# An attention and coupling block on one core: the softmax scale moved into the f16 split of q and k

## What is computed

```
x = x + layernorm(attention(layernorm(x)))
x = x + layernorm(coupling_cycles(layernorm(x)))        # 3 cycles of a small network with gelus

# attention: 16 heads of width 64, segments of 128 rows, carried memory M and normaliser Z
scores  = (q @ k.T) * (1 / sqrt(64))                    # per head and segment, 128 x 128
scores  = where(upper triangle, -inf, scores)
att_dot = softmax(scores) @ v
att_mem = (elu(q) + 1) @ M / ((elu(q) + 1) @ Z.T)
M, Z    = M + (elu(k) + 1).T @ v,  Z + sum(elu(k) + 1)
out     = (gate * att_mem + (1 - gate) * att_dot) @ Wo
```

## Time and profile before

| | |
|---|---|
| median of three runs | 1298.55 us |
| lowest and highest | 1297.96, 1299.42 us |
| profiled execution, first to last instruction (span) | 1296.2 us |
| TensorE matmul, busy | 1091.5 us, 84% |
| VectorE, busy | 913.4 us, 70% |
| ScalarE, busy | 596.7 us, 46% |
| POOL (GpSimd), busy | 582.6 us, 45% |
| mean granted clock of TensorE | 0.946 |

### The profile page before, as it was taken

One profiled execution on the slowest core, in us unless ns is written; L12 is line 12 of the kernel. 1 busy time (PEld: TensorE's weight loads), 2 busy tenths in 40 slices (PEclk: granted clock), 3 DMA queues, 4 the chain that ended last, 5 costly groups with the idle time before them and its releaser, 6 DMA issues.

```text
span 1296.2 us, 20762 instructions
## 1 busy us (share of the span) xinstructions
PE 1091.5 (84%) x7108; PEld 764.7 (59%) x7172; DVE 913.4 (70%) x1668; ACT 596.7 (46%) x1255; POOL 582.6 (45%) x715
## 2 busy tenths in 40 slices
PE   3798889886989898878888888798989779999992
PEld 1476657564767575647676756576767665433431
DVE  4868686876686868657878786868686754444486
ACT  4344444544454444443535354445444543444463
POOL 2145454544454545434545454545454552222274
PEclk9899999988899999989999999989999888999996
DMA  5000000000000000000000000000000010300033
GB/s 159 20 9 9 10 9 11 8 14 6 10 9 9 9 9 10 10 10 10 9 9 9 9 10 9 9 9 9 9 1 9 1 28 1 138 0 0 1 65 65
DMA packets 14681, 24.00 MB, mean 19 GB/s; under 512 B 5104, under 2 KB 6896, under 8 KB 14064
## 3 DMA queue, kind: packets, MB, share of 16 engines
q1 hardware_dynamic: 14576, 22.63, 5.7%
HBM read 13.97 MB, written 8.65 MB: 17 GB/s over the span
## 4 chain that ended last, share of the span: by engine, by line
PE 41%; DVE 38%; issue 11%; ACT 6%; POOL 2%; DMA 1%; DVEq 1%; SPq 0%; POOLq 0%; ACTq 0%
DVE arena L769 10%; PE ps L1172 9%; PE ps L1067 8%; PE ps L1278 6%; DVE arena L867 3%; PE ps L1125 3%; DVE arena L788 3%; ACT arena L555 3%; PE ps L1291 3%; DVE arena L819 2%; PE ps L1112 2%; DVE arena L713 2%; DVE arena L801 2%; DVE arena L779 2%; DVE arena L782 2%
## 5 line engine op out<-in xcount | busy, mean ns | idle before, releaser
L1067 PE MATMUL ps<-arena 128*128 128x512 f16 x1152 | 270.8, 386 | 6.0 <-DVE arena L745 4.2
L555 ACT ACTIVATE arena<-ps,arena 128x128 f32<-128x128 f32 x512 | 140.7, 381 | 252.4 <-DVE arena L791 251.3
L769 DVE STREAM_TRANSPOSE arena<-ps 128x1024 f32<-128x1024 f32 x96 | 189.8, 1979 | 35.4 <-PE ps L1067 35.4
L1067 PEld LDWEIGHTS ps<-arena 128*128 128x128 f16 x1152 | 113.1, 100 | 129.4 <-issue 14.0
L402 POOL TENSOR_TENSOR arena<-arena 128x256 f32<-128x256 f32 x128 | 93.1, 728 | 153.3 <-DVE arena L801 153.3
L1125 PEld LDWEIGHTS ps<-arena 128*128 128x128 f32 x1024 | 135.7, 202 | 29.5 <-issue 21.2
L1125 PE MATMUL ps<-arena 128*128 128x65 f32 x1024 | 139.2, 281 | 16.2 <-DVE arena L801 15.0
L386 POOL TENSOR_TENSOR arena<-arena 128x512 f32<-128x512 f32 x64 | 81.2, 1268 | 135.4 <-ACT arena L548 135.2
L1112 PE MATMUL ps<-arena 128*128 128x128 f32 x512 | 84.5, 303 | 45.6 <-ACT arena L555 45.5
L1172 PE MATMUL ps<-arena 128*128 128x256 f32 x544 | 122.0, 382 | 0.3 <-ACT arena L567 0.3
L372 POOL TENSOR_TENSOR arena<-arena 128x2 f32<-128x2 f32 x50 | 9.8, 196 | 230.8 <-DVE arena L709 230.8
(11 more groups left out here) (110 smaller groups left out, 1920.9 us busy)
## 6 DMA issues: line engine op xcount, KB each, us to landing
x_rows<-arena SPq DMA_DIRECT2D x17, 256.0 KB, 2.0
arena<-in_L_attn_x_dram SPq DMA_DIRECT2D x64, 64.0 KB
arena<-x_rows SPq DMA_DIRECT2D x4, 1024.0 KB, 7.9
out_dram<-arena SPq DMA_DIRECT2D x32, 128.0 KB, 2.9
arena<-in_L_attn_Wq_dram SPq DMA_DIRECT2D x1, 1024.0 KB, 12.3
arena<-in_L_attn_Wk_dram SPq DMA_DIRECT2D x1, 1024.0 KB, 14.4
arena<-in_L_attn_Wv_dram SPq DMA_DIRECT2D x1, 1024.0 KB, 17.4
arena<-in_L_attn_Wo_dram SPq DMA_DIRECT2D x1, 1024.0 KB, 13.0
```

The source lines that it names most:

```text
L555: last = act.activation(Pr[:, par, j, :], s_bank[:, par, j * P:(j + 1) * P], ACT.Exp, scale=SCALE, bias=shift[:, par, j:j + 1])
L769: dve.transpose(dst[:, d0:d0 + 32, :], bank.rearrange("p w (d c) -> p d w c", c=C)).then_inc(x_free, 1)
L1067: last = pe.matmul(bank[:, w, :], xc[:, lx, k, w * P:(w + 1) * P], W16[lw][:, k, i, :], start=(n == 0), stop=(n == 5))
```

## The change

The scale 1/8 is applied as 1/2 on q and 1/4 on k where they are split into f16 parts. The copies of the high parts get the factor as their scale. The subtractions of the low parts become T * factor - high, as `scalar_tensor_tensor`. The scores then come scaled out of TensorE. The multiply of L791, its buffer `shift` and the wait before it go away, the exponential has no scale but its default and takes `negm` as its bias, and `m_done` counts two signals for each group. elu(q)+1 is made from the unscaled q as before.

```diff
-SCALE = DK ** -0.5
+Q_SCALE, K_SCALE = 0.5, 0.25
+assert Q_SCALE * K_SCALE == DK ** -0.5
...
-        shift = alloc(GU).rearrange("p (h j) -> p h j", h=2)
...
-                    act.activation(qhT[g % 2].rearrange("p j i -> p (j i)"), t_bank[b], ACT.Copy).then_inc(qk_act, 1)
+                    act.activation(qhT[g % 2].rearrange("p j i -> p (j i)"), t_bank[b], ACT.Copy,
+                                   scale=Q_SCALE).then_inc(qk_act, 1)
...
-                    act.activation(khT[g % 2].rearrange("p j i -> p (j i)"), t_bank[b], ACT.Copy).then_inc(qk_act, 1)
+                    act.activation(khT[g % 2].rearrange("p j i -> p (j i)"), t_bank[b], ACT.Copy,
+                                   scale=K_SCALE).then_inc(qk_act, 1)
...
-                        act.wait_ge(m_done, bp * 64 + (4 * G + 2 * par + 2))
+                        act.wait_ge(m_done, bp * 32 + (2 * G + par + 1))
                         for j in range(GP):
                             last = act.activation(Pr[:, par, j, :], s_bank[:, par, j * P:(j + 1) * P], ACT.Exp,
-                                                  scale=SCALE, bias=shift[:, par, j:j + 1])
+                                                  bias=negm[:, par, j:j + 1])
...
-                    dve.tensor_tensor(f(qlT[g % 2]), T, f(qhT[g % 2]), ALU.subtract).then_inc(t_free[b], 1)
+                    dve.scalar_tensor_tensor(f(qlT[g % 2]), T, Q_SCALE, f(qhT[g % 2]), ALU.mult,
+                                         ALU.subtract).then_inc(t_free[b], 1)
...
-                    dve.tensor_tensor(f(klT[g % 2]), t_bank[b], f(khT[g % 2]), ALU.subtract).then_inc(t_free[b], 1)
+                    dve.scalar_tensor_tensor(f(klT[g % 2]), t_bank[b], K_SCALE, f(khT[g % 2]), ALU.mult,
+                                         ALU.subtract).then_inc(t_free[b], 1)
...
-                        dve.wait_ge(m_done, bp * 64 + (4 * G + 2 * par + 1))
-                        dve.tensor_scalar(shift[:, par, :], negm[:, par, :], SCALE, None,
-                                          ALU.mult).then_inc(m_done, 1)
```

## The result

The changed kernel takes 1285.86 us (median; 1283.12 to 1286.9) against 1298.26 us of the kernel before on the same chip: a ratio of 0.9896, interval 0.9878 to 0.9915. It is faster by 12.4 us (11.0 to 15.8 by the interval); the forecast was 17.7. The profiled execution took 1285.42 us, with a span of 1283.6 us where it was 1296.2.

What follows compares the result with a forecast made beforehand. It took the attention stage to be bound by a path changing between TensorE and VectorE. Groups 0, 3 and 2 gave 9.2 + 4.3 + 4.2 = 17.7 us off, forecasting 1281 us, range 1274 to 1288 (1271 to 1291 with neighbours).

Steps and rivals of the forecast that it cites:

- The swaps at nothing: 128 subtractions as scalar_tensor_tensor on VectorE and 128 scaled copies on ScalarE were taken to cost nothing more.
- The slower rival: New subtractions wait for POOL, up to 0.56 us more for each of 96 on the path: 1308 us, chance 0.03.
- the long multiplies: Line 791's long multiplies wait for a POOL instruction, through the port pair VectorE shares with GpSimd; removal takes these waits away.
- Group 0, 0.70 us in twelve steps: Transpose of line 769 starts 0.70 us earlier, then held by TensorE's projection; with 0.8 in the last step, 9.2 us.
- The gain then goes down the VectorE chain: Group 0's gain passes along VectorE to the read-out and the output projection on TensorE, which had waited for VectorE.
- Group 3, the multiply itself: Path runs reduction, multiply, exponentials, TensorE's transposes; gain 0.20 us eleven times, 0.43 four times, about 0.4 last: 4.3 us.
- Group 1, nothing: No gain: the transpose behind waits 1.66 us for TensorE's projection anyway, and TensorE has other work before needing the exponentials.
- Group 2, 4.2 us: About 0.9 us in one full-clock step, nearly nothing in eleven with TensorE late at lower clock, the rest at pair ends.
- The spacing of 0.60 between reductions: Two reductions back to back on VectorE cost 1.20 us; standing 0.68 apart, group 2 would gain some 0.7 us less.
- All of VectorE's saving counts: Rival: TensorE moves up too in group 0 and its slow stretch leaves group 2: 1273 us, chance 0.13.
- The next limit stands just behind: Rival: late TensorE or ScalarE takes back most of the gain of groups 0 and 2: 1290 us, chance 0.14.
- a widening only: TensorE's slow stretches may meet other work, 7 us to either side, 1274 or 1288; counted in the forecast's range.

Runs made afterwards that it cites:

- second experiment: Changed kernel with the 128 multiplies still made on VectorE but read by nobody, exponentials waiting for the reduction alone: 1307.34 us, ratio 1.0058.
- first experiment: Changed kernel with the multiply (factor 1) and its wait put back, exponentials taking its result: 1300.05 us, ratio 1.0001.
- sixth experiment: Changed kernel with a tiny unused SBUF reduction on VectorE behind the two reductions of group 0: 1282.05 us, ratio 0.9876.
- fourth experiment: Changed kernel with group 2's memory additions moved ahead of the division of its second half, except in a pair's last step: 1280.34 us, ratio 0.9860.
- eighth experiment: Changed kernel with extra mask products on TensorE in two waits, five before group 1's scores, eight between group 0's memory updates: 1272.03 us, ratio 0.9791.
- the filled kernels: Changed kernel and kernel before, each with five and eight extra mask products in the same two TensorE waits: 1272.03 us and 1297.06 us.

## Why the prediction was right, and where its steps failed

The time lies in the range and 4.9 us above the number. That the gain is what the multiplies had held back holds, by VectorE's earlier release in groups 0 and 2. ScalarE's earlier start gave nothing in the ordinary steps of group 3, and by itself it cost time (second experiment). The sizes of all four groups were off, and that the total came near is in part luck.

*The swaps at nothing:* right. 684 and 685 ns, 592 ns, and the first experiment at 1.0001. The slower rival, subtractions that run into POOL, is out. What the prediction says of the long multiplies fits all of them in the profile before: 51 of the 128 took over 0.25 us, and each of these ended within 0.12 us of the end of a POOL instruction that it had run beside. But 54 of the 77 short ones ran beside one too.

*Group 0, 0.70 us in twelve steps:* the limit named was right (line 771 starts 1.73 behind the first reduction and waits for the projection), and 0.30 of it was given back on the next two instructions. "The gain then goes down the VectorE chain" failed: it took the chain behind line 771 as rigid. Removing an instruction also removed its read, and with it what the next read is compared with. The sixth experiment shows it, 0.73 a step with the read put back. In the last step 1.1 came instead of 0.8, and in the first steps of pairs 1 and 2, where nothing was forecast, 0.38 and 0.30 were lost, with 4.8 us of group 0 at the lower level in each instead of 3.

*Group 3, the multiply itself:* this step failed. "The path goes reduction, multiply, exponentials, transposes on TensorE" was read from the chain that ended last. That chain gives one predecessor for each instruction. Line 1084 has two, the exponentials by way of line 1112 and the banks by line 819, and the load at 431.71 shows the second with 0.19 us of waiting. The forecast didn't weigh that row. In place of 0.20 a step the gain was 0.00, and 0.2 to 0.6 when the banks came free earlier (fourth experiment). The 1.5 us of the table come from two pair ends, and what made them stays open.

*Group 1, nothing:* failed, with the sign against the change. VectorE is as late as I said. But TensorE's wait there grew from 1.36 to 1.74 us, and its matmuls then ran at half clock in four or five more steps, 1.02 us each, some 5 us. The prediction had allowed slow stretches 7 us to either side, without saying where they would go.

*Group 2, 4.2 us:* too small by 8.5, the largest miss. "Whatever VectorE saves here, TensorE is late" took the low stretch of the earlier trace rows as belonging to group 2. The sum of the low stretches stayed (109 us before, 113 after, from 40 to 1070 us), and part of it moved from group 2 (70 us, then 50) to groups 0 and 1 (18 us, then 35). In the five ordinary steps with a loss in group 1 (2, 4, 8, 10 and 13) group 2 gains 1.28 us in the mean, and in the seven others it gains 0.48; in the second execution of the changed kernel it is 1.23 in four and 0.34 in eight. How much moves is not fixed: there group 2 kept 63 us. With TensorE kept at its clock every step of group 2 gains (eighth experiment). And "nothing" was too low even at the lower level: steps 5, 9 and 14 have 3.4 us of it in group 2 before and after the change, and gain 0.6 to 0.7. That it is the same stretch that moved is read from the traces and wasn't tried by itself. Groups 1 and 2 together: forecast 4.2, measured 7.2.

*The spacing of 0.60 between reductions:* right, two of them take 1.28 to 1.29 us where one takes 0.678. The rule weighed there, by which they would stand 0.68 apart, is for instructions that are held: "VectorE: DVE Perf Modes" of the Trainium skill, section The DRAIN you can't avoid, itself adds that an instruction that is not held starts earlier. By the spacings the reductions weren't held, and the transpose of line 868 was.

*The rivals.* "All of VectorE's saving counts" is half true with the clock kept up (23.6 us of span between the filled kernels): 0.9 us a step in group 2 as it says, but not in group 0, where TensorE's projection stays the limit. "The next limit stands just behind" describes group 3, not the whole. The one that mattered was in the text as a widening only: the slow stretches stood behind TensorE's waits of 1.7 us and more, so it could have been looked for at these places.

*What stays open:* why filling group 1's wait alone gave a mean clock of 0.942 in one execution and 0.950 to 0.954 in three; what the second fill would give alone; why the second transpose of line 868 changes with the hold; and which step loses the clock.

## What to carry to other kernels

For each engine that a change lets go earlier, ask for all the predecessors of what it releases, the PSUM banks that must be empty among them, and read the short waits of 0.2 us: one of them marked a second limit that stood right behind the first. Then ask where TensorE will now wait longer and where it waits already, since such a wait can cost clock in the work behind it; matmuls put into two of these waits were worth more in the changed kernel (14 us) than the change itself (12), and only 4 us in the kernel before. And when an instruction is removed from VectorE, look at what partitions the ones around it read.

## What the runs showed of the hardware

Exponentials that start earlier, with VectorE's load unchanged, made this kernel slower by 7.3 us (1307.34 against 1300.05). TensorE's granted clock fell from its upper level, 2.4 GHz, to the lower, 1.2 GHz (0.51), behind the wait of group 1 the more often the longer the wait was: in none of 52 steps with a wait up to 1.42 us, in 6 of 38 with 1.69 to 1.79, in 18 of 41 with 1.80 to 2.06, in 12 of 13 with 2.17 to 2.38, and in none with the wait filled. Up to 13 extra matmuls a step, 36 us more of work in the stage, took the low stretches from 113 to 51 us and shortened the kernel by 14 us. A transpose of VectorE that reads SBUF from partition 0 started 2.01 us behind the one before it when the last read of SBUF had started at partition 64, and 1.83 when a read of two columns from partition 0 stood in between.
